# Biases off TensorE, and moments taken ahead of scaling, in a one-core perceiver kernel

## What is computed

```
L0: two multi-head attentions with MLPs (a1: self, masked; a2: cross on the context), then rotary
    self-attention with an inner norm (l0a), then 8 experts top 2 + shared (l0f)
L1: one-head cross attention (l1x), a recurrence over time (l1a), experts of capacity 128 (l1f)
L2: 16-head cross attention (l2x), rotary self-attention (l2a), 8 experts + a shared one (l2f):
    y += c[:, e] * ((silu(x @ W1 + B1) * (x @ W3 + B3)) @ W2 + B2)
L3: 16-head cross attention (l3x), self-attention (l3a), 16 experts + shared (l3f)
```

## Time and profile before

| | |
|---|---|
| median of 3 runs | 2368.74 us |
| the profiled execution | 2372.82 us, span 2371.1 us |
| TensorE matmul, busy | 2126.9 us, 90% of the span |
| TensorE weight load | 1783.4 us, 75% |
| VectorE | 1378.1 us, 58% |
| ScalarE | 1121.6 us, 47% |
| GpSimd | 489.7 us, 21% |
| mean granted TensorE clock | 0.922 of 2.4 GHz |

### The profile page before, as it was taken

How to read it: one execution, slowest core, us unless ns; L and a number is a source line. 1 busy time by engine, 2 the same in 40 slices (tenths; PEclk the granted TensorE clock), 3 DMA queues, 4 the chain that set the end, 5 groups by cost and what they waited for, 6 DMA issues and landing times. The chain is left out here.

```text
span 2371.1 us, 42159 instructions
## 1 busy us (share of the span) xinstructions
PE 2126.9 (90%) x15112; PEld 1783.4 (75%) x15112; DVE 1378.1 (58%) x2694; ACT 1121.6 (47%) x2248; POOL 489.7 (21%) x402
## 2 busy tenths in 40 slices
PE   4775999999887998579899999987989999999898
PEld 1553999999545885267699999956758999997577
DVE  6453777777325444731577777734446777775366
ACT  1232666666322442321466666523336666664244
POOL 2222222221011430100322222011322222220034
PEclk9687999999895998689999999997989999999789
DMA  4144010100031213421110100002211101000022
GB/s 204 31 187 156 30 43 30 43 28 0 36 141 44 79 60 132 182 110 61 74 43 30 43 28 28 0 16 71 78 73 43 44 29 42 28 14 0 18 70 80
DMA packets 32315, 145.34 MB, mean 61 GB/s; under 512 B 3760, under 2 KB 9136, under 8 KB 28848
## 3 DMA queue, kind: packets, MB, share of 16 engines
q1 hardware_dynamic: 32176, 143.53, 16.7%
HBM read 126.90 MB, written 13.90 MB: 59 GB/s over the span
## 5 line engine op out<-in xcount | busy, mean ns | idle before, releaser
L1001 ACT ACTIVATE pTh<-ps 128x512 fp32r<-128x512 f32 (+1 forms) x768 | 354.0, 520 | 384.0 <-PE ps L901 381.9
L1059 DVE TENSOR_TENSOR pTl<-ps,pTh 128x512 fp32r<-128x512 f32 (+1 forms) x768 | 415.7, 582 | 129.1 <-ACT pTh L1001 128.9
L601 PE MATMUL ps<-pTh,ch 128*128 128x256 f32 (+1 forms) x1248 | 383.4, 307 | 2.3 <-DVE pTl L1059 2.3
L602 PE MATMUL ps<-pTl,ch 128*128 128x256 f32 (+1 forms) x1248 | 348.3, 279 | 0.0
L603 PE MATMUL ps<-pTh,cl 128*128 128x256 f32 (+1 forms) x1248 | 348.1, 279 | 0.0
L601 PE MATMUL ps<-cTh,qh 128*128 128x512 f32 (+2 forms) x768 | 276.8, 360 | 15.2 <-POOL ql L855 8.1
L603 PE MATMUL ps<-cTh,ql 128*128 128x512 f32 (+2 forms) x768 | 269.1, 350 | 0.0
L602 PE MATMUL ps<-cTl,qh 128*128 128x512 f32 (+2 forms) x768 | 268.5, 350 | 0.0
L1046 DVE TENSOR_REDUCE top<-ps 128x1 f32<-128x802 f32 x192 | 189.4, 986 | 110.8 <-PE ps L603 110.8
L601 PEld LDWEIGHTS ps<-pTh,ch 128*128 128x128 f32 (+1 forms) x1248 | 235.1, 188 | 16.2 <-DVE pTl L1059 12.3
L602 PEld LDWEIGHTS ps<-pTl,ch 128*128 128x128 f32 (+1 forms) x1248 | 235.7, 189 | 0.0
(11 more groups left out here) (344 smaller groups left out, 3675.5 us busy)
## 6 DMA issues: line engine op xcount, KB each, us to landing
w<-l1f_w_in SPq DMA_DIRECT2D x16, 1024.0 KB, 8.4
raw<-ctxT_in SPq DMA_DIRECT2D x16, 801.0 KB, 4.3
raw<-ctx_in SPq DMA_DIRECT2D x14, 832.0 KB, 4.4
wg<-l0f_guide_in SPq DMA_DIRECT2D x10, 704.0 KB, 5.2
z<-ctx_in SPq DMA_DIRECT2D x8, 832.0 KB, 12.8
z<-z SPq DMA_DIRECT2D x8, 832.0 KB, 11.7
keys<-ctx_in SPq DMA_DIRECT2D x8, 832.0 KB, 10.5
zT<-zT SPq DMA_DIRECT2D x8, 801.0 KB, 14.7
```

Source lines behind the costliest of these rows:

```text
L601: pe.matmul(out, high, moving_high, start=start, stop=False)
L602: pe.matmul(out, high, moving_low, start=False, stop=False)
L1001: nc.scalar.activation(pTh[0:w, PARTS[g][0]:PARTS[g][0] + n, slot, :], ps[0:w, turned_bank[slot][g], 0:n * P].rearrange("p (k r) -> p k r" ...
L1059: dve.tensor_tensor(pTl[0:w, at, slot, :], ps[0:w, turned_bank[slot][g], 0:n * P].rearrange("p (k r) -> p k r", r=P), pTh[0:w, at, slot, : ...
```

## The change

1. Bias rows leave TensorE. Packs hold biases spread over all partitions. A new `bias_on_pool(dst, src, row)` adds one to all four tiles with a single GpSimd operation between two blocks: ahead of a1's, l0a's, l2a's and l3a's self_attention, ahead of a2's and l2x's late_values, ahead of l1x's one_head_attention and l1f's expert block, and in a1's and a2's tail ahead of the MLP's dense products: ten in all. GpSimd now also waits for weights.
2. The value bias of l0a and l3a is added by `keep_out`, feature chunk by feature chunk.
3. In l0a's rotary stage VectorE works out the rotated bias once, and adds it to `crossed` in each tile.
4. In l2f the biases of all experts are one product: TensorE turns `combine`, VectorE keeps it, TensorE multiplies it by the nine bias rows, VectorE adds the result to x ahead of the first second_product.
5. In rows_to_norms VectorE takes tile t and its moments before it scales tile t - 1 (with two norms, the second norm lags one tile more); TensorE turns tile t - per - 1 behind product t; ScalarE makes its square roots ahead of copying a turned tile.

```diff
+                        if t >= per + 1:
+                            turn_tile(pe, t - per - 1, norms[-1][1], 4 + t - per - 1, z_ready, turned_ready)
+                    for t in range(NT - per - 1, NT):
+                        turn_tile(pe, t, norms[-1][1], 4 + t, z_ready, turned_ready)
...
+                    for step in range(NT + per - 1):
                         for n in range(per):
+                            if 0 <= step - n < NT:
+                                count += 1
+                                deviation(act, step - n, count, var_ready, std_ready)
+                        if step >= per + 1:
+                            keep_turned(act, step - per - 1, 4 + step - per - 1, turned, turned_ready)
...
+                    for step in range(NT + per):
+                        if step < NT:
+                            dve.wait_ge(product_ready, step + 1)
+                            link(products[step][4](nc.vector, ps[:, step, 0:D]))
+                            moments(step, 0)
+                        for n in range(per):
+                            t = step - 1 - n
+                            if 0 <= t < NT:
+                                last = apply(t, n)
+                                if n < per - 1:
+                                    link(last)
+                                    moments(t, n + 1)
+                                else:
+                                    last.then_inc(z_ready, 1)
...
-                if row is not None:
-                    terms.append((ones[0:1, :], row))
...
                         def keep_out(t):
                             act.wait_ge(out_turned, t + 1)
+                            if columns is not None:
+                                for c in range(chunks):
+                                    last = nc.scalar.activation(oT[:, c, t * P:(t + 1) * P], ps[:, 6, (2 + c) * P:(3 + c) * P],
+                                                                ACT.Identity, bias=columns[:, c:c + 1])
+                                last.then_inc(out_kept, 1)
+                                return
...
+                        def turn_combine():
+                            pe.wait_ge(combine_ready, 1)
+                            for t in range(NT):
+                                last = pe.transpose(ps[0:count, 4 + t, D:D + P],
+                                                    combine[:].rearrange("p (e t) -> p t e", t=NT)[:, t, :], ident[:])
+                            last.then_inc(combine_turned, 1)
+
+                        def biases():
+                            pe.wait_ge(combine_kept, 1)
+                            for t in range(NT):
+                                last = pe.matmul(ps[:, 4 + t, D:2 * D], combineT[:, t, :], down_bias, start=True, stop=True)
+                            last.then_inc(biases_ready, 1)
...
+                            if down_bias is not None and first:
+                                (biases if slot else turn_combine)()
 
                         def second_product(e, slot, turn_, first):
+                            if down_bias is not None and first:
+                                pe.wait_ge(biases_added, 1)
...
-                                if bias:
-                                    last = pe.matmul(ps[:, 4 + t, 0:D], ones[0:1, :],
-                                                     wd[slot][0:1, chunks * D:(chunks + 1) * D],
-                                                     start=False, stop=True)
...
+                            if down_bias is not None and first and slot == 0:
+                                dve.wait_ge(combine_turned, 1)
+                                dve.tensor_copy(combineT[:], ps[0:count, 4:8, D:D + P]).then_inc(combine_kept, 1)
+                            elif down_bias is not None and first:
+                                dve.wait_ge(biases_ready, 1)
+                                dve.tensor_tensor(x[:], x[:], ps[:, 4:8, D:2 * D], ALU.add).then_inc(biases_added, 1)
+                                dve.wait_ge(biases_added, 1)
...
+                            if biases:
+                                dve.wait_ge(turned_by, per * t + 2)
+                                dve.tensor_tensor(crossed[:, t % 2, :], crossed[:, t % 2, :], offset[:], ALU.add)\
+                                    .then_inc(turned_by, 1)
...
+        def bias_on_pool(dst, src, row):
+            nc.gpsimd.tensor_tensor(dst[:], src[:], row.unsqueeze(1).broadcast_to([P, NT, D]), ALU.add)
...
+                    bias_on_pool(mid, inner, w("li1_b"))
                     self_attention(qT, kT, v, oT, HP ** -0.5, HP, maskT=w("later"))
...
+                bias_on_pool(mid, inner, w("li1_b"))
                 late_values(w("wv"), q, oT, HP, sums, beta=w("lny_b"))
```

More of the change, by code:

```diff
@@ L371, in _ @@
                     link = Chain(dve, chain)
[L372 to L379, removed]
+                    turn = {}
@@ L1249, in expert_weights, with experts @@
                                     down_high, down_low, room, fetch_guide, fetch_down, split_first)
-        def experts(held, router, routed, kind, count, hidden, bias=False, norm=True):
+        def experts(held, router, routed, kind, count, hidden, down_bias=None, norm=True):
+            bias = down_bias is not None
             chunks = -(-hidden // P)
@@ L1618, in rotary_projections @@
                 wide = sb("wide", [P, 2, 2, H, HP], where=own)
+                offset, part = (sb(n, [P, 2 * D], where=own) for n in ("offset", "part"))
+                per = 4 if biases else 3
                 wqk, wv = w.chunks("wqk", KC), w.chunks("wv", KC)
@@ L1631, in rows @@
                             if t >= 2:
-                                pe.wait_ge(turned_by, 3 * (t - 1))
+                                pe.wait_ge(turned_by, per * (t - 1))
                             for k in range(KC):
                                 last = pe.matmul(ps[:, t % 2, :], xT[:, k, t * P:(t + 1) * P], wqk[:, k, :],
-                                                 start=(k == 0), stop=not biases and k == KC - 1)
-                            if biases:
-                                last = pe.matmul(ps[:, t % 2, :], ones[0:1, :], w("bqk", 1), start=False, stop=True)
+                                                 start=(k == 0), stop=(k == KC - 1))
                             last.then_inc(rows_ready, 1)
@@ L1644, in values @@
                                 last = pe.matmul(ps[:, 2 + t % 2, 0:D], xT[:, k, t * P:(t + 1) * P], wv[:, k, :],
-                                                 start=(k == 0), stop=not biases and k == KC - 1)
-                            if biases:
-                                last = pe.matmul(ps[:, 2 + t % 2, 0:D], ones[0:1, :], w("bv", 1), start=False, stop=True)
+                                                 start=(k == 0), stop=(k == KC - 1))
                             last.then_inc(values_ready, 1)
@@ L1960, in context_normaliser, with inner_attention @@
                                         store_rows, turn)
-        def inner_attention(name, rotary, biases, out_row, finish, norms, first_split):
+        def inner_attention(name, rotary, biases, out_row, before, after, norms, first_split):
             weights_here(name)
@@ L1972, in inner_attention @@
                 oT = sb("oT", [P, KC, N], where=tmp)
-                values = values_by_head(xT, w.chunks("wv", KC), v, dh, row=w("bv", 1) if biases else None)
+                values = values_by_head(xT, w.chunks("wv", KC), v, dh)
                 def count_column(pool):
@@ L1983, in inner_attention @@
                           + values, pool=count_column)
-                self_attention(qT, kT, v, oT, dh ** -0.5, dh)
-                rows_to_norms(token_rows(oT, w.chunks("wo", KC), finish, row=w(out_row, 1)), norms, [(xT, None, None)],
-                              pool=first_split)
+                bias_on_pool(after, before, w(out_row))
+                self_attention(qT, kT, v, oT, dh ** -0.5, dh, columns=w("bv") if biases else None)
+                rows_to_norms(token_rows(oT, w.chunks("wo", KC), lambda t: plus(after[:, t, :], after[:, t, :])), norms,
+                              [(xT, None, None)], pool=first_split)
         def many_head_cross(name, dh, scale, row):
@@ L2456, in columns, with rows @@
     return v.reshape(-1, P).T
-def row(v):
-    out = np.zeros((P, v.size), np.float32)
-    out[0] = v.reshape(-1)
+def rows(w):
+    out = np.zeros((P, w.shape[1]), np.float32)
+    out[0:w.shape[0]] = w
     return out
```

133 lines of the change are left out of this document (83 added, 50 removed).

## The result

The changed kernel took 2298.62 us (median of 4 runs, 2286.42 to 2300.33) beside 2369.07 for the kernel before: ratio 0.9695, 95% interval 0.9656 to 0.9733. The forecast was 2318, its range 2302 to 2338, so the kernel became faster by more than was said, and just beyond the range. The profiled execution took 2297.8 us, span 2296.0: 75.1 less than before, where the forecast's sum was 50.7 less.

The account below looks back on a forecast made before the run. Long stretches were read as TensorE at full speed, short stages as chains over four engines with TensorE waiting most for VectorE's scaled tile. Terms summed to -50.7 us, from 2372.8 to 2322.1, adjusted to 2318; range 2302 to 2338.

Parts of the forecast that it names:

- Clock: New TensorE holes in l2f and late_values may each bring a half-clock stretch: +1.5 us (0 to +8).
- attention of l0a and l3a: keep_out with a bias column becomes two activations instead of one: +3.3 us over both stages (0 to +3.6).
- l3a, l2a and l1x: Short rows_to_norms stages, l3a's at half clock, gain from removed biases: -4.3, -4.0 and -2.5, together -10.8 us.
- a2's first product: Stage running half at half clock: biases worth 3.0 us, less 0.3 at its end: -2.7 us.
- better than the terms: Rival: half-clock stages end early enough to keep the clock, and a1 gains 6: 2304 us, chance 0.04.
- TensorE-bound with one norm: -2.2 each: a1's first, a2's second, l1f, l2x: four biases save 2.5 us, the end costs 0.3; together -8.8.
- Two norms: a1's second product and l0a: VectorE's waits fill and biases go, -4.5 and -3.0, together -7.5 us.
- late_values, +4.1: a2 and l2x: GpSimd's 2.35 us addition goes ahead of the memset, delaying VectorE and TensorE: +4.1 us.
- Rotary projections: l0a's TensorE work there loses its row and value biases, VectorE adds the offset: -5.2 us (-6 to -3).
- the loop's other bound: Rival: l2f's expert loop meets another bound at some 10 us an expert, 11 less gained: 2329 us, chance 0.12.
- half clock in it: Rival: TensorE gets half clock in l2f's loop, nine experts 75 us longer: 2393 us, chance 0.04.
- additions that cost at each block: Rival listed as GpSimd, its statement partly cut: the GpSimd additions cost time at blocks; chance 0.08.

Follow-up runs that it names:

- two pairs of traces: Profiles of the kernel before and the changed kernel, then of both again without edit: -75.1 and -74.5 us; on repeat 2367.19 us (trace) and 2292.22 us (median).
- fill_l0a: Changed kernel plus three 128x256 matmuls a tile, results unread, in l0a's output stage: 2292.33 us.
- order_only: Kernel before with only the new order of rows_to_norms, all biases still on TensorE: 2358.03 us, ratio 0.9976.
- late_behind: Changed kernel with GpSimd's additions of a2 and l2x behind late_values' own GpSimd work instead of ahead: 2296.42 us, ratio 0.9708.
- biases_only: Changed kernel with the old order of rows_to_norms, biases still off TensorE: 2313.95 us, ratio 0.979.
- l2f_rows_back: Changed kernel with l2f's bias matmuls back on TensorE for each expert and tile, without the combine product: 2313.87 us, ratio 0.979.
- experiment 3: Changed kernel with l2f's bias matmuls put back on TensorE: 2313.87 us, ratio 0.979.
- experiment 7: Unread matmuls added: l0a's output stage of the changed kernel, 2292.33 us; self_attentions, with a2's and l2x's additions in cross_attention's tail, 2299.9 (one a tile), 2300.11 (three).
- experiments 1 and 2: Each half of the rows_to_norms change alone: biases off TensorE with the old order 2313.95 us; new order on the kernel before 2358.03 us.

## Why the prediction was wrong

**The step that failed is "Clock", +1.5.** The terms were worked out at the clock that each stage had in one trace, and the clock was then charged only for new holes. It went the other way: 41 to 49 us less at 1.2 GHz, 12 to 15 us. It is seen where code is unchanged (-6.5 and -2.3 in the two pairs of traces), in the attention of l0a and l3a (-4.6 and -4.2 instead of +3.3; at equal clock keep_out costs what I said) and in part in l3a, l2a and l1x (-15.8 and -18.7 instead of -10.8). There it is the change and not the execution. l1x's and l3a's output stages and l0a's attention repeat within 0.1 us in the two traces of each kernel, 12.3, 16.9 and 29.0 us before, 8.3, 10.1 and 25.5 after: -4.1, -6.7 and -3.5, where the terms gave -2.5, -4.3 and +1.65. (VectorE's shorter tile, below, has a part in the first two.) I held the clock of these stages fixed under a change that moved it. a2's first product (-7.4 instead of -2.7) is another case: it gave -3.3 in the second pair, so most of its miss is the one execution that I had read. That trace of before was itself among those with the lowest clock, 0.922 where 35 executions have a median of 0.925; I took its time 4.1 us above the median, which allows for this in the total but not in the stages. My rival "better than the terms", 2304 at a chance of 0.04, had this mechanism, with too small a price and too small a chance.

**"TensorE-bound with one norm: -2.2 each" was mis-sized.** l1f measures -3.2 at full clock: 0.75 a bias instead of 0.62, and no 0.3 lost at the end. For l2f I had noted that the matmul behind a bias also starts late, and priced 0.8 there; the same holds here. l1f's takes are 3.46 us apart where I said 3.8, and l3a's value rows agree: they gave -1.5 instead of -2.5 only because their clock fell from 1.00 to 0.92, and at 1.00, in fill_l0a's trace, they take 18.45 us instead of 21.68, 0.81 a bias. Over four stages this is 4 us, of which the first pair of traces shows 1.2, because a1's first and l2x's ran at a lower clock than before (0.79 against 0.89, 0.88 against 0.92). In the second trace l2x's is at 1.00 and takes 17.93 us, 4.5 less than before. The second pair's -16.1 is too much in turn: 5.4 of it is a1's first, which ran at 0.76 before and 0.86 after.

**"Two norms" and the short stages: VectorE's tile was too long.** 1.52 us instead of 1.75, since the inverse starts 0.10 us behind bn_aggr. a1's second product went from 32.09 to 26.17 at the same clock: -5.9 instead of -4.5, of which order_only has -4.9, at a clock of 0.90. l1a and l3x, put at 0, gave -2.7 (order_only: 10.13 and 12.60 us, so it is the order). Together some 5 us.

**late_values, +4.1, was right in its wait and wrong in its follow-up.** At full clock the two stages are 2.14 and 2.3 us longer. Behind the wait a stretch at half clock made one or both longer still in both traces of the changed kernel (+8.3 in l2x; +3.1 in a2 with +1.0 in l2x) and in late_behind's (+3.5 in a2). In three other traces with the same wait (biases_only, l2f_rows_back, fill_l0a) neither stage took longer than its wait, and in no trace without the wait did either take longer than before. So the wait seems to bring the risk and not the stretch itself.

**What held.** l2f: an expert at 8.35 us (8.4 forecast), the wait for the added biases 2.16, the block -23.6 (-22.1), -22.5 by experiment 3; between the second traces it is -19.1, with a clock of 0.97 before and 0.90 after. Rotary projections -5.4 (-5.2), in part by luck: their clock fell from 0.93 to 0.84, and late_behind's trace has 18.95 us at 0.91, 6.5 less than before. keep_out +1.7 a stage. Of the rivals, the loop's other bound, half clock in it (0.95 granted) and additions that cost at each block did not occur. VectorE was held by GpSimd, but in l0a's output stage (1.91 us at 712.28, where the form takes 0.48), not in the rotary one. It was held there before the change too, 1.90 us at 742.08, so this is no cost of the change.

**What stays open.** Which stages meet the half clock in a given execution was not controlled, so the split between the clock's 12 to 15 us and the terms' 8 to 11 is from the fit and not from a kernel held at one clock. What makes the clock rise in stages from which work was taken is not shown: experiment 7 raised it in most stages by adding work. How much of the gain needs both halves of the change is open too (experiments 1 and 2).

## What to carry to other kernels

Where a profile shows short stages at a mixed clock, compare two traces of the same kernel before pricing them: what differs is the execution's. Give the clock of the rest a term that can be a gain: here the change returned a fifth to a quarter more than its fixed-clock sum. Price a small matmul by a stage with and without it, not by its own row. Before an operation goes to an idle GpSimd, look at what stands behind it there and at VectorE's operations with two SBUF inputs beside it; the tail of a long block showed no cost, the head of a short one cost nearly the full 2.35 us (2.14 and 2.3).

## What the hardware did that was not expected

- The clock of one stretch differs between executions of one kernel: 27.47 us at 0.60 and 20.16 at 0.92 with the same instructions. Most stretches (34 and 31 of 52) repeat within 0.1 us.
- GpSimd kept VectorE out over two of its operations: VectorE's sum began at 1507.21 beside the copy and stayed through the addition that followed, 3.32 us for 0.22 of work.
- More work on TensorE went with a higher clock in most stages (0.58 to 0.74, 0.77 to 1.00), and with a lower one in others: 0.71 to 0.61 in l2a's attention with three matmuls a tile, 0.65 to 0.58 in l3a's with one.
